# Out-projection rows of a head spread over the units of a slot in chunks one, two and four, and the next chunk's input loaded from ScalarE's queue

## Chip, cores and metric

One core of a Trainium2 chip. The metric is the device time of one execution in microseconds, as the median over the runs of the kernel.

## The reference

x is 2048 tokens by 512, float32. xn is x with LayerNorm. The result is x + attention(xn) + ffn(xn). The attention has 16 heads, a latent of rank 128 shared by keys and values, and a rotary part of 64:

```
q = xn @ wq.T                      # per head 128 nope + 64 rotary
kv = xn @ wkv_a.T                  # 128 latent + 64 rotary key
q_lat = q_nope @ wkv_b[h, :128]    # per head, into the latent
kv_cache = rmsnorm(kv_lat, kv_norm_w)
scores = (q_lat @ kv_cache.T + q_pe @ k_pe.T) * SCALE, causal
out_lat = softmax(scores) @ kv_cache
out = (out_lat @ wkv_b[h, 128:]) of all heads @ wo.T
ffn = xn @ w_ste.T + bias          # w_ste: ternary weight times its mean size
```

## The kernel before, in words

`build_prepare` makes, chunk by chunk, the transposed input, keys and values, the linear part and the products of the weights (Wq for a head's latent query, Wp for the rotary part of a pair of heads, Wv for value times output), and stores xT, the linear part with the residual (acc), Wq, Wp and Wv in scratch memory. `build_attention` is where the change lies. Every factor is held as a high and a low part, so each product is three matmuls (five for scores).

**Order of the work.** There are four chunks of 512 query tokens (NCH = 4, four blocks of 128 rows each, QB = 4), and in each chunk 16 heads (H = 16): 64 heads g, written out in full. A head works in slots. In chunks one and two a slot s is a whole head (s = g, s = 0 to 31); in chunks three and four a head takes two slots of two row blocks each (s = 32 to 95). The functions at the head of the file (L128 to L209) give each piece of work its slot and its unit. A slot has rows times chunk number units: 4 in chunk one, 8 in chunk two, 6 in chunk three, 8 in chunk four. In every unit every engine runs through the same list, so the order on each queue is fixed, and engines meet through semaphores.

**One unit on TensorE** (`slot` in `block.tensor`): `scores` of one row block against 512 keys into one of three p_score buffers (L1106, mask at L1110); `project_rotary` (L1086, p_rot) for the heads g+1 and g+2 if the slot opens an odd head (in chunk one ahead of the scores); `project_latent` parts (L1086, p_lat) of the next head; `project_out` (L1138, p_result), the out-projections of head s-2 or s-3, one per row block; `values` (L1126, p_out), the PV product of slot s-2 in groups. `project_out` of row i waits until row i-2 has been accumulated, since p_result has two buffers, and for row 0 for Wv (`wv_in`) and for o_l of the head (`o_split`).

**VectorE**: `copy_scores` (L1178, with maxima, L1184), `turn_row` (L1200, 32 by 32 transposes of a row after its exp), `rotate` (L1212, L1216, five operations on p_rot), `split_query` (L1223), `split_output` (L1227), `accumulate` (L1241, acc). **ScalarE**: `exp_row` (L1283), `high_group` (L1304), `high_output` (L1310), `high_query` (L1321), `high_rotary` (L1328), and the DMA issues of the last quarter of an exchange (L1293) and of Wq (L1315). **GpSimd**: `add_rotary` (L1369), `low_rotary` (L1378, L1381), `low_group` (L1389).

**SyncE** (`block.sync`) issues, in each slot s in this order: two quarters of the exchange of slot s-1 (L991: eight DMAs of transposed probabilities from turned to pT, after the last `turn_row`), Wp (L998) in slots that open an odd head, in chunk one the load of Wv for the next head (L1003), the third quarter of the exchange (four DMAs), and from slot 16 on the load of Wv here. At the end of a slot that closes head 14 of a chunk come the tables of the next chunk (L1013, L1014) and xT (L1008), at the end of one that closes head 1 of a chunk the store of the chunk before (L1018) and the load of the residual of this one (L1023). `load_v` of head g+1 waits until all four rows of head g are projected. xT, Wq, Wp, Wv and acc have one buffer each. A wait on SyncE holds everything behind it.

The out-projections of a head stand: in chunk one in unit 1, all four rows, in slot g+3; in chunk two in units 6, 6, 7, 7 of slot g+2; in chunk three in units 2 to 5; in chunk four in units 0, 1, 2, 2.

Of the kernel before, what the change touches and what calls it, by code (L numbers as in the profile page):

```python
# [32 lines left out]
H = 16  # L33
# [123 lines left out]
def out_heads(s):  # L157

    if s < H:
        return (s - 3,) if s >= 3 else ()  # L160
    if s < 2 * H:
        return (s - 3, s - 2) if s == H else (s - 2,)
    if s == 2 * H + 1:
        return (2 * H - 2,)
    return (s // 2 + H - 2,) if s % 2 == 0 and s > 2 * H else ()


def out_unit(s, g, i):
    if s < H:
        return 1  # L170
    if s < 2 * H:
        return 0 if g == s - 3 else 6 + i // 2
    return 0 if s % 2 else (2 + i if phase(s) == 2 else (0, 1, 2, 2)[i])
# [14 lines left out]

def rotate_ops(s, u):
    if phase(s) == 0:  # L190
        return range(5) if u == 0 else ()
    first = rotary_unit(s) + 1
    return ((0,), (1, 2), (3, 4))[u - first] if first <= u <= first + 2 else ()


def rotary_unit(s):
    return 1 if phase(s) == 3 else 0


def rotary_add_unit(s):  # L200
    return (1, 4, 4, 5)[phase(s)] if opens_head(s) else None


def rotary_high_unit(s):
    return (2, 5, 5, 6)[phase(s)] if opens_head(s) else None
# [680 lines left out]
def build_attention(nc, t, keep, stored):  # L886
    with ExitStack() as ctx:
# [95 lines left out]
        def _(sp):  # L983
# [21 lines left out]
            def load_chunk(j):  # L1005

                sp.wait_ge(lat_projected, H * j)
                sp.dma_start(xT[:, :, :, :].bitcast(F32), t["xT_scr"][j]).then_inc(xT_in, 16)  # L1008

# [15 lines left out]
            def slot(s):  # L1025
                if 1 <= s <= SLOTS:
                    exchange(s - 1, (0, 1))
# [8 lines left out]
                if s < SLOTS and closes_head(s):  # L1036
                    j, h = chunk_of(head_of(s)), head_of(s) % H
                    if j + 1 < NCH and h == H - 2:
                        load_tables(j + 1)
                        load_chunk(j + 1)  # L1040
# [4 lines left out]
            def load_next_v(s):  # L1045
                for g in out_heads(s):
                    if g + 1 < HEADS:
                        load_v(g + 1)
# [14 lines left out]
        def _(pe):  # L1063
# [77 lines left out]
            def slot(s):  # L1141
                g = head_of(s) if s < SLOTS else HEADS
                for u in range(units_of(s)):
                    rotary = u == rotary_unit(s) and opens_head(s) and g % 2 and g + 1 < HEADS
# [24 lines left out]
        def _(dve):  # L1169
# [75 lines left out]
            def slot(s):  # L1245
                g = head_of(s) if s < SLOTS else HEADS
                for u in range(units_of(s)):
# [9 lines left out]
                    if opens_head(s) and g % 2 and g + 1 < HEADS:  # L1257
# [19 lines left out]
        def _(act):  # L1277
# [33 lines left out]

            def load_q(g):
# [18 lines left out]
            def slot(s):  # L1331
                g = head_of(s) if s < SLOTS else HEADS
                for u in range(units_of(s)):
# [9 lines left out]
                    if u == query_unit(s) and g + 1 < HEADS:  # L1343
                        high_query(g + 1)
                        if g + 2 < HEADS:
                            load_q(g + 2)
                    if u == rotary_high_unit(s) and g + 1 < HEADS:
# [7 lines left out]
            for i in range(2):  # L1355
                act.wait_ge(stored["wq"][i], 16 * H // 2)
            load_q(1)
# [138 lines left out]
```

## Time and profile before

| | |
|---|---|
| median of 3 runs | 1896.98 us |
| lowest, highest | 1886.88, 1898.66 us |
| the profiled execution, its own time | 1894.48 us |
| its span, first to last instruction | 1892.0 us |
| mean granted TensorE clock | 0.969 |
| TensorE, VectorE, ScalarE, GpSimd busy | 91%, 64%, 45%, 53% |

The profile is of one execution. Times in its rows are microseconds from the span's start. The four chunks of attention begin at about 190, 450, 800 and 1260 us; what lies before is `build_prepare`, which the change does not touch.

### The profile page before, as it was taken

What the parts mean: (1) busy time and instruction counts of PE and PEld (TensorE: products, weight loads), DVE (VectorE), ACT (ScalarE), POOL (GpSimd) and SP (SyncE); (2) the same over time, 40 slices, a digit from 0 to 9 for tenths busy, and PEclk for the clock granted to TensorE, in tenths of its full rate; (3) what the DMA queues carried; (4) which work ended last, traced back from release to release, by engine and by line L of the source; (5) the groups of instructions that cost most, each with busy time, mean ns of one, the idle gap of its engine ahead of it and who ended that gap; (6) DMA issues with size and microseconds to landing.
All of it is one profiled execution on the core that took longest, in us unless ns stands there. A gap on an engine that the chain in (4) does not pass through costs nothing.

```text
span 1892.0 us, 28195 instructions
## 1 busy us (share of the span) xinstructions
PE 1717.4 (91%) x9326; PEld 1452.8 (77%) x9326; DVE 1211.1 (64%) x2801; ACT 850.7 (45%) x1358; POOL 1008.2 (53%) x635
## 2 busy tenths in 40 slices
PE   6988788878899999799999999979999999999996
PEld 5877666656778877578888888868888888888875
DVE  4674466655666677466776776657666666666663
ACT  4554334433344454345445445434544544454442
POOL 4674444442365556355655655635555565664654
PEclk9898899988999999899999999989999999999998
DMA  6995355563756656656555554555665564655543
GB/s 201 362 329 198 102 151 146 158 190 101 201 148 174 170 156 163 182 150 179 158 149 145 158 149 135 162 166 143 175 162 130 150 162 119 166 143 130 148 121 105
DMA packets 127184, 309.12 MB, mean 163 GB/s; under 512 B 29442, under 2 KB 41987, under 8 KB 125508
## 3 DMA queue, kind: packets, MB, share of 16 engines
q1 hardware_dynamic: 98720, 233.33, 43.1%
q10 hardware_dynamic: 28324, 74.05, 15.0%
q8 instruction: 72, 1.18, 0.3%
q14 instruction: 68, 0.56, 0.1%
HBM read 113.28 MB, written 34.60 MB: 78 GB/s over the span
## 4 chain that ended last, share of the span: by engine, by line
PE 62%; issue 11%; DVE 7%; POOL 4%; ACT 3%; DMA 1%; SPq 1%; ACTq 1%; POOLq 0%; DVEq 0%
PE p_score L1106 25%; PE p_out L1126 18%; PE p_result L1138 7%; PE p_lat L1086 7%; PE p_rot L1086 5%; POOL pT L1389 2%; DVE acc L1241 2%; DVE turned L1200 2%; ACT qp_h L1328 1%; DVE rot_sin L1216 1%; DVE probs L1178 1%; SPq L991 1%; POOL qp_l L1378 1%; POOL qp_l L1381 1%; PE p_score L1110 1%
## 5 line engine op out<-in xcount | busy, mean ns | idle before, releaser
L1389 POOL TENSOR_TENSOR pT<-pT,pT_h 128x1024 fp32r<-128x1024 f32 x320 | 688.6, 2178 | 445.5 <-ACT pT_h L1304 442.8
L1178 DVE TENSOR_SCALAR_CACHE_REDUCE probs<-p_score 128x512 f32<-128x512 f32 (+3 forms) x640 | 383.6, 602 | 433.6 <-PE p_score L1106 256.8
L1283 ACT ACTIVATE probs<-probs,neg_max 128x128 f32<-128x128 f32 (+15 forms) x256 | 307.9, 1203 | 453.8 <-DVE neg_max L1184 430.3
L1304 ACT ACTIVATE pT_h<-pT 128x1024 fp32r<-128x1024 f32 x320 | 291.1, 963 | 267.3 <-PE p_out L1126 203.6
L1200 DVE STREAM_TRANSPOSE turned<-probs 128x1024 f32<-128x1024 f32 (+7 forms) x384 | 341.8, 915 | 43.2 <-ACT probs L1283 38.5
L1126 PE MATMUL p_out<-pT_h,V_h 128*128 128x256 f32 (+3 forms) x1024 | 303.4, 296 | 18.7 <-POOL pT L1389 18.7
L1126 PE MATMUL p_out<-pT,V_h 128*128 128x256 f32 (+3 forms) x1024 | 302.7, 296 | 0.0
L1126 PE MATMUL p_out<-pT_h,V_l 128*128 128x256 f32 (+3 forms) x1024 | 302.3, 295 | 0.0
L1106 PE MATMUL p_score<-Kp,qp_h 128*128 128x512 f32 (+3 forms) x640 | 235.9, 369 | 15.6 <-POOL qp_l L1381 15.6
L1106 PE MATMUL p_score<-Kn_h,q_h 128*128 128x512 f32 (+3 forms) x640 | 240.3, 375 | 2.4 <-DVE q_l L1223 2.4
L1138 PE MATMUL p_result<-Wv,o_h 128*128 128x512 f32 x512 | 173.8, 421 | 70.9 <-DVE acc L1241 51.4
L1106 PE MATMUL p_score<-Kn_l,q_h 128*128 128x512 f32 (+3 forms) x640 | 234.9, 367 | 0.0
L1106 PE MATMUL p_score<-Kn_h,q_l 128*128 128x512 f32 (+3 forms) x640 | 234.4, 366 | 0.0
L1106 PE MATMUL p_score<-Kp,qp_l 128*128 128x512 f32 (+3 forms) x640 | 233.6, 365 | 0.0
L1086 PE MATMUL p_lat<-xT,Wq 128*128 128x512 f32 x768 | 225.2, 410 | 0.0
L1126 PEld LDWEIGHTS p_out<-pT_h,V_h 128*128 128x128 f32 x1024 | 196.7, 192 | 35.7 <-issue 18.7
L1126 PEld LDWEIGHTS p_out<-pT_h,V_l 128*128 128x128 f32 x1024 | 196.4, 192 | 13.1
L1241 DVE SCALAR_TENSOR_TENSOR acc<-p_result,inv_sum,acc 128x512 f32<-128x512 f32 x256 | 184.6, 745 | 28.5 <-PE p_result L1138 20.7
L1126 PEld LDWEIGHTS p_out<-pT,V_h 128*128 128x128 f32 x1024 | 196.1, 192 | 4.2
L1378 POOL TENSOR_TENSOR qp_l<-rotated,qp_h 64x512 fp32r<-64x512 f32 x64 | 82.3, 1285 | 196.6 <-ACT qp_h L1328 192.7
L1138 PEld LDWEIGHTS p_result<-Wv,o_h 128*128 128x128 f32 x512 | 89.9, 194 | 111.4 <-DVE acc L1241 68.3
L1086 PEld LDWEIGHTS p_lat<-xT,Wq 128*128 128x128 f32 x768 | 142.1, 195 | 25.0
(135 smaller groups left out, 2384.7 us busy)
## 6 DMA issues: line engine op xcount, KB each, us to landing
pT<-turned SPq DMA_DIRECT2D x384, 128.0 KB, 3.6
Wq<-wq_scr ACTq DMA_DIRECT2D x63, 512.0 KB, 4.8
Wv<-wv_scr SPq DMA_DIRECT2D x63, 512.0 KB, 3.5
pT<-turned SPq DMA_DIRECT2D x192, 112.0 KB, 3.8
pT<-turned SPq DMA_DIRECT2D x192, 96.0 KB, 2.9
pT<-turned ACTq DMA_DIRECT2D x128, 128.0 KB, 3.9
Wp<-wp_scr SPq DMA_DIRECT2D x31, 512.0 KB, 4.4
pT<-turned SPq DMA_DIRECT2D x192, 80.0 KB, 2.6
```

The lines of the kernel that those rows point to most:

```text
L991: sp.dma_start(slots(pT[s % 2][32 * a:32 * (a + 1), :], s)[:, r, 0:tiles, :, :].bitcast(F32), slots(turned[s % 2][32 * r:32 * (r + 1), :], ...
L1086: mm = pe.matmul(out, weights[:, w, it, :], xT[:, x, it, :], start=(it == 0 and k == 0), stop=(it == IT - 1 and k == 2))
L1106: mm = pe.matmul(out[:, 0:width], q[p][:, rows], kk[:, keys], start=(k == 0), stop=(k == 4 and b < j))
L1126: mm = pe.matmul(out[:, :, cols, :], v[:, t, :], pt[:, :, t - first, rest, :], start=(t == 0 and a == 0), stop=(t == piece_tiles(s) - 1 an ...
L1138: mm = pe.matmul(out[:, :], o[:, rows], Wv[:, w, :], start=(k == 0), stop=(k == 2))
L1178: dve.tensor_scalar(probs[row % ROW_RING][:, b * CW:b * CW + width], p_score[n % SCORE_RING][:, 0:width], SCALE, LOWEST, ALU.mult, ALU.max ...
L1200: last = dve.transpose(to.rearrange("p a t q -> p t a q"), rows.rearrange("p (t a q) -> p t a q", a=4, q=32))
L1241: dve.scalar_tensor_tensor(out=acc[:, i, :], in0=p_result[(QB * g + i) % 2][:, :], scalar=inv_sum[g % 4][:, i:i + 1], in1=acc[:, i, :], op ...
L1283: act.activation(probs[row % ROW_RING][:, 0:width], probs[row % ROW_RING][:, 0:width], ACT.Exp, bias=neg_max[p][:, i:i + 1], scale=1.0, ac ...
L1304: act.activation(high.rearrange("p r t i q -> p r t (i q)"), low.bitcast(F32).rearrange("p r t i q -> p r t (i q)"), ACT.Copy).then_inc(p_ ...
L1378: pool.tensor_tensor(qp_l[p][0:ROPE, :], rotated[own, :], qp_h[p][own, :].bitcast(F32), ALU.subtract).then_inc(qp_ready, 1)
L1389: pool.tensor_tensor(low.rearrange("p r t i q -> p r t (i q)"), low.bitcast(F32).rearrange("p r t i q -> p r t (i q)"), high.bitcast(F32). ...
```

## The change

Out-projection rows of a head are given other units: chunk one 1, 1, 2, 3 instead of 1, 1, 1, 1; chunk two units 6 and 7 of slot g+2 and units 0 and 1 of slot g+3 instead of 6, 6, 7, 7 (so `out_heads` names two heads in slots 16 to 31, slot 32 gets the last two rows of head 29, and Wv is asked for by the slot of the last row); chunk four 0, 1, 3, 4 instead of 0, 1, 2, 2. The rotary projection moves to unit 2 in chunk three (3 in slot 62, the last before chunk four), and to unit 1 in slots 15 and 31; the operations that follow it move along, in chunk three partly into the next slot. xT of the next chunk is loaded by ScalarE right behind the Wq load of the next chunk's first head, instead of by SyncE at the end of the slot of head 14, and the tables are loaded at the start of that head's first slot.

```diff
@@ out_heads
     if s < 2 * H:
-        return (s - 3, s - 2) if s == H else (s - 2,)
+        return s - 3, s - 2
+    if s == 2 * H:
+        return (2 * H - 3,)
     if s == 2 * H + 1:
@@ out_unit
     if s < H:
-        return 1
-    if s < 2 * H:
-        return 0 if g == s - 3 else 6 + i // 2
-    return 0 if s % 2 else (2 + i if phase(s) == 2 else (0, 1, 2, 2)[i])
+        return (1, 1, 2, 3)[i]
+    if s == H and g == s - 3:
+        return i // 2
+    if s <= 2 * H:
+        return (None, None, 0, 1)[i] if g == s - 3 else (6, 7, None, None)[i]
+    return 0 if s % 2 else (2 + i if phase(s) == 2 else (0, 1, 3, 4)[i])
@@
+def rotary_unit(s):
+    return (1 if s == H - 1 else 0, 1 if s == 2 * H - 1 else 0, 3 if s == 4 * H - 2 else 2, 1)[phase(s)] if opens_head(s) else None
+
 def rotate_ops(s, u):
+    if not opens_head(s):
+        return ()
     if phase(s) == 0:
-        return range(5) if u == 0 else ()
+        return range(5) if u == rotary_unit(s) else ()
     first = rotary_unit(s) + 1
+    if s == 4 * H - 2:
+        return ((0, 1), (2, 3, 4))[u - first] if first <= u <= first + 1 else ()
     return ((0,), (1, 2), (3, 4))[u - first] if first <= u <= first + 2 else ()
-def rotary_unit(s):
-    return 1 if phase(s) == 3 else 0
 def rotary_add_unit(s):
-    return (1, 4, 4, 5)[phase(s)] if opens_head(s) else None
+    if phase(s) == 2:
+        return 0 if not opens_head(s) else None
+    return rotary_unit(s) + (1, 4, None, 4)[phase(s)] if opens_head(s) else None
 def rotary_high_unit(s):
-    return (2, 5, 5, 6)[phase(s)] if opens_head(s) else None
+    if phase(s) == 2:
+        return 1 if not opens_head(s) else None
+    return rotary_unit(s) + (2, 5, None, 5)[phase(s)] if opens_head(s) else None
@@ block.sync
-            def load_chunk(j):
-
-                sp.wait_ge(lat_projected, H * j)
-                sp.dma_start(xT[:, :, :, :].bitcast(F32), t["xT_scr"][j]).then_inc(xT_in, 16)
             def slot(s):
+                if opens_head(s) and head_of(s) % H == H - 2 and chunk_of(head_of(s)) + 1 < NCH:
+                    load_tables(chunk_of(head_of(s)) + 1)
...
                     j, h = chunk_of(head_of(s)), head_of(s) % H
-                    if j + 1 < NCH and h == H - 2:
-                        load_tables(j + 1)
-                        load_chunk(j + 1)
                     if j and h == 1:
                         store_chunk(j - 1)
                         load_residual(j)
             def load_next_v(s):
                 for g in out_heads(s):
-                    if g + 1 < HEADS:
+                    if g + 1 < HEADS and out_unit(s, g, QB - 1) is not None:
                         load_v(g + 1)
@@ block.scalar
+            def load_chunk(j):
+
+                act.wait_ge(lat_projected, H * j)
+                act.wait_ge(rot_projected, H // 2 * j)
+                act.dma_start(xT[:, :, :, :].bitcast(F32), t["xT_scr"][j]).then_inc(xT_in, 16)
...
                         if g + 2 < HEADS:
                             load_q(g + 2)
+                        if (g + 2) % H == 0 and g + 2 < HEADS:
+                            load_chunk(chunk_of(g + 2))
...
+            act.wait_ge(stored["xT"], 16 * (NCH - 1))
             load_q(1)
```

In `block.tensor` and `block.vector` the test for the slot of an odd head is adapted to the new `rotary_unit`; nothing else changes there.

## Rows read from the trace of the kernel before

**Rows 1.** The page's head and view 1, busy time and share of the span

```profile
span 1892.0 us, 28195 instructions
...
PE 1717.4 (91%) x9326; PEld 1452.8 (77%) x9326; DVE 1211.1 (64%) x2801; ACT 850.7 (45%) x1358; POOL 1008.2 (53%) x635
```

**Rows 2.** TensorE's waits over the whole span: us in total, times, longest us

```profile
PE p_result L1138 <- DVE acc L1241: 51.4, 49, 3.2
PE p_rot L1086 <- issue: 29.5, 3, 11.2
```

**Rows 3.** Stretches: us, then PE, PEld, DVE, ACT, POOL busy, PEclk, DMA, GB/s

```profile
354.00:384.50 30.50, 25.86 (x133) 20.60 (x133) 20.01 (x51) 12.73 (x28) 13.67 (x10) 1.00 0.57 156
384.50:417.20 32.70, 28.38 (x133) 22.56 (x131) 20.11 (x52) 12.80 (x28) 13.21 (x9) 0.90 0.54 147
562.80:604.40 41.60, 40.01 (x198) 33.08 (x197) 29.14 (x68) 20.32 (x32) 23.23 (x14) 1.00 0.61 164
```

**Rows 4.** A rotary projection in the chain of waits; then TensorE in chunk one

```profile
353.95 2.81 PE p_rot L1086 x12
...
363.90 0.73 PE L1138 MATMUL p_result<-Wv,o_h 128*128 128x512 f32 x2 [3.03 <-DVE acc L1241]
...
372.48 0.33 PE L1106 MATMUL p_score<-Kp,qp_h 128*128 128x128 f32 x1 [1.06 <-POOL qp_l L1381]
```

**Rows 5.** VectorE in the same slot (timeline)

```profile
359.73 2.79 DVE L1216 TENSOR_TENSOR rot_sin<-p_rot,sinT_sb 32x512 f32<-32x512 f32 x4
```

**Rows 6.** GpSimd in chunk one, odd slot and even slot (timeline)

```profile
363.82 3.65 POOL L1389 TENSOR_TENSOR pT<-pT,pT_h 128x1024 fp32r<-128x1024 f32 x2
...
378.57 3.65 POOL L1389 TENSOR_TENSOR pT<-pT,pT_h 128x1024 fp32r<-128x1024 f32 x2 [6.14 <-ACT pT_h L1304]
```

**Rows 7.** SyncE in an even slot of chunk two, and TensorE at row 0

```profile
625.36 0.33 SPq L1003 DMA_DIRECT2D Wv<-wv_scr  x1
629.18 9.12 SPq L991 DMA_DIRECT2D pT<-turned  x12
...
639.73 0.62 PE L1138 MATMUL p_result<-Wv,o_h 128*128 128x512 f32 x2
```

**Rows 8.** TensorE's waits in chunk two, 470 to 770

```profile
PE p_result L1138 <- DVE acc L1241: 12.7, 15, 1.4
PE p_out L1126 <- POOL pT L1389: 4.5, 1, 4.5
```

**Rows 9.** DMA issues, median us to landing: all Wv; one Wp

```profile
Wv<-wv_scr SPq DMA_DIRECT2D x63, 512.0 KB, 3.5
...
Wp<-wp_scr SPq DMA_DIRECT2D x1, 512.0 KB, 6.9
```

**Rows 10.** SyncE at the store of chunk one; ScalarE waiting for an exchange

```profile
494.73 0.40 SPq L1018 DMA_DIRECT2D out<-acc  x1
...
500.21 9.37 SPq L991 DMA_DIRECT2D pT<-turned  x12
...
518.59 2.95 ACT L1304 ACTIVATE pT_h<-pT 128x1024 fp32r<-128x1024 f32 x3 [8.40 <-DMA pT<-turned]
```

**Rows 11.** XT issues (SyncE), Wq issues (ScalarE), p_rot, third and fourth chunk

```profile
771.31 0.43 SPq L1008 DMA_DIRECT2D xT<-xT_scr  x1
...
1232.77 0.43 SPq L1008 DMA_DIRECT2D xT<-xT_scr  x1
...
763.91 0.34 ACTq L1315 DMA_DIRECT2D Wq<-wq_scr  x1
...
1227.31 0.35 ACTq L1315 DMA_DIRECT2D Wq<-wq_scr  x1
...
782.33 4.67 PE L1086 MATMUL p_rot<-xT,Wp 128*128 128x512 f32 x12 [11.25 <-issue]
...
1244.46 5.46 PE L1086 MATMUL p_rot<-xT,Wp 128*128 128x512 f32 x12 [9.32 <-issue]
```

**Rows 12.** TensorE in an even slot of chunk four (timeline)

```profile
1425.26 0.73 PE L1138 MATMUL p_result<-Wv,o_h 128*128 128x512 f32 x2 [0.94 <-DVE acc L1241]
```

More of the change, by code:

```diff
@@ L1143, in slot @@
                 for u in range(units_of(s)):
-                    rotary = u == rotary_unit(s) and opens_head(s) and g % 2 and g + 1 < HEADS
+                    rotary = u == rotary_unit(s) and g % 2 and g + 1 < HEADS
                     if rotary and s < H:
@@ L1256, in slot @@
                             split_output(old)
-                    if opens_head(s) and g % 2 and g + 1 < HEADS:
+                    if g % 2 and g + 1 < HEADS:
                         for op in rotate_ops(s, u):
```

## The prediction

> **What bounds the kernel now.** I read the busy shares first, then TensorE's own waits, then TensorE's timeline of one steady pair of heads in each chunk, and only then the queues. TensorE is busy 91% of a span of 1892.0 us [rows 1], so only its idle time and its slow stretches can be won. Its two largest waits are both touched by the change [rows 2]: the out-projection waits for VectorE's accumulate (51.4 us, 49 times), and the rotary projection waits at the three chunk changes for xT (29.5 us in 3 waits; the releaser reads "issue" because it is a DMA). The first has one cause everywhere: p_result has two buffers, and four rows are projected in one or two units, so row 2 needs row 0 accumulated. A third cost is the clock: two neighbouring pairs of chunk one take 30.5 us at clock 1.00 and 32.7 us at 0.90 [rows 3], so a dip costs 2.2 us.
>
> I call a slot with a rotary projection odd, the other even. Twelve 512-column matmuls take 2.81 us [rows 4], so 0.23 us each: one out row 0.7 us, one full score unit 1.15 us.
>
> **Part 1, chunk one, rows at units 1, 1, 2, 3.** In the odd slot TensorE waits 3.03 us for acc and ends by waiting 1.06 us for qp_l at the next head [rows 4]. VectorE gets to the accumulates only after the rotate operations, whose four rot_sin alone hold it from 359.73 for 2.79 us [rows 5]. That order stays. TensorE now does score 2 and two latent parts (2.4 us) before row 2, so of 3.03 us about 0.8 is left. But then comes the PV product, and its pT is not there: GpSimd starts it at 363.82, 3.65 us for two groups [rows 6], so the first is usable at about 366.2 against TensorE's 364.6: 1.6 us of new wait. The slot ends 0.9 us sooner, the next head's qp_l, whose chain hangs on latent parts finished 4 us sooner but behind pT on GpSimd, comes 1.6 us sooner. In the even slot the wait before row 2 was 0.2; row 3 leaves the stretch ahead of the PV product, and pT (start 378.57, behind ScalarE's exchange issues [rows 6]) is then 1.6 us late instead of 0.3. Per pair: 1.6 won, 0.7 given back, 0.9 net; six pairs give -5.5. If pT is not the next limit, 3.2 per pair. Wv is asked for later, at unit 3, with 4 us before its use; the middle landing of Wv is 3.5 us [rows 9]: I allow +2. Three pairs had a dip of 2.2; gaps half as long should spare half: -3.5. Sum -7, bounds -20 and +6.
>
> **Part 2, chunk two, rows at units 6, 7, 0, 1.** The 12.7 us of acc waits in this chunk [rows 8] go. But Wv has one buffer. Before, its load was issued at the end of a slot (625.36) and had 14 us until row 0 at unit 6 (639.73). Now head g ends at unit 1 of the slot after, and SyncE asks for Wv of g+1 behind the exchanges, which begin at 629.18 and take 9.12 us to issue [rows 7]. VectorE reaches the transpose that releases them about 1.4 us sooner than now (one accumulate fewer ahead of it, then ScalarE's last exp sets it): 627.8 + 9.1 = 636.9, and Wv lands L later. Row 0 is due at 639.73 less the acc wait of 0.73 that went, 639.0. Even slots wait L - 2.1; odd slots, 2.5 us longer but with Wp to issue too, L - 4 less the wait before them. L: the median of all Wv loads is 3.5 us; a 512 KB load on SyncE's queue between exchanges (Wp) took 6.9 [rows 9]. I take 4.3, nearer the first, since all exchanges are issued before it and only the last are still moving: 2.2 us in each even slot, none in odd ones. Five steady even slots and slot 17: 11.5 - 12.7 = -1, bounds -7 and +26 (at L = 6.9 both kinds of slot wait, 6.4 us per pair).
>
> **Part 3, slot 18.** store_chunk(0) stands at the end of SyncE's slot 17 and waits for all 64 accumulates. Rows 2 and 3 of head 15 now come in slot 18, units 0 and 1, so the store goes from 494.73 to about 498.8. Behind it on SyncE's queue: residual, twelve exchanges (from 500.21 for 9.37 us), then Wv for head 16. The exchanges landed at 518.6, when ScalarE's 8.40 us wait ended [rows 10], and cost TensorE 4.5 us [rows 8]. Now they land about 4 us later, and Wv, which head 16 needs at unit 6 (about 508), comes with or after them, at about 522. TensorE stands 14 us, then does 8.4 us of work, some of it at the low clock (+3), up to where it stood before at 524: +10, bounds +3 and +16. This stall takes the place of the wait of 4.5.
>
> **Part 4, xT from ScalarE's queue.** Before, xT stood on SyncE behind Wv and tables: issued 771.31 and 1232.77, in use 782.33 and 1244.46 [rows 11]: about 11 us. The new place is right behind the Wq load, which ScalarE issued at 763.91 and 1227.31 [rows 11]. ScalarE's own waits cost nothing: both counts stand when Wq is issued.
> Into the third chunk: xT lands at about 775 (11 us). The rotary comes at unit 1, after a score and an out row, and with the Wv wait of slot 30 it is due at about 772. Before it began at 782.33: -7.3, and its slow product (4.67 us against 2.81) probably a normal one: -8.5 in all; bounds -4 and -10.
> Into the fourth chunk: landing 1238 to 1240; the rotary moves from unit 0 to unit 3 of slot 62, three scores and an out row later, due 1235.1 + 4.3 = 1239.4. The 9.3 us go, and 5.46 becomes about 2.8: -11.5, bounds -6 and -12.
> Into the second chunk: Wq and xT go out only 2 us sooner. Wait 29.5 - 11.2 - 9.3 = 9.0 shrinks to about 5: -3.8. In the same slot 15 an acc wait of 3 us and half a dip go, since the rotary sits later: -4.5. Together -8, bounds -2 and -11.
> The exchange DMAs that now queue behind xT on ScalarE are needed a slot later: nothing. The tables are asked for a slot sooner on SyncE, idle then: nothing.
> In sentences of their own: the Trainium skill, "DMA: Bandwidth & Descriptors", section "Issuing engines are not separate DMA queues", says that transfers issued from different engines run on the same 16 engines and interleave, so that a second queue saves only the issue time. By it the exchanges, which stood behind xT on one queue, now take a share beside it, and the sum would be rival B's; by the rows above it is mine.
>
> **Part 5, rotary of chunk three from unit 0 to 2.** Same products, still ahead of row 0; VectorE's rotate operations fall among accumulates and end about 2 us later; exchanges 1.5 us later, with about 2 us of slack ahead of PV. The o_l waits (1.2 us per pair) are not touched. 0, bounds -2 and +8.
>
> **Part 6, chunk four, rows at units 0, 1, 3, 4.** Even-slot waits of 0.94 [rows 12] and 0.3 per pair. Unit 3's score is narrow (0.55 us), so row 2 still waits about 0.5: 0.75 won in each of seven pairs, and 1 at the chunk's start: -6.5, bounds -10 and 0. One 0.7 wait in slot 32: -0.7.
>
> **Sum.** -7 - 1 + 10 - 8.5 - 11.5 - 8 - 6.5 - 0.7 = -33.2. Waits removed one by one tend to come back in part: in this schedule SyncE's issue time fills most of a slot, and I worked out only the next-latest cause. I take three quarters, -25 (my choice, from no row). The profiled execution took 1894.48 us, the median of three is 1896.98: 1897 - 25 = 1872 us.
>
> **Rivals.**
> A. The forecast: 1872.
> B. xT from ScalarE lands late because SyncE's exchanges move beside it instead of behind it. At xT's rate (2 MB in 11 us) the up to 1.5 MB of twelve exchanges are 8 us of transfer; half of it in xT's way makes 15 us, and the three chunk changes win 2, 4.5 and 6 less: 1872 + 12.5 = 1885. For it: twelve exchanges are being issued from before 1227 on. Against: they are issued 0.75 us apart and land in 3 to 4 us, so they leave gaps.
> C. The other side: Wv is late all through chunks one and two. It decides at L = 4.7: from there odd slots wait too, and each later us is paid twice per pair. At 6.9 chunk two gives +26 instead of -1, chunk one loses 2.8 per pair, +17, and slot 18 comes to its upper bound, +6: 1872 + 50 = 1922; at 5.5 about 1890. For it: Wp among exchanges took 6.9; against: the load is the last on its queue.
> D. The Wv load is nearly in time (L = 3.3: 5 less) and slot 18 costs its lower bound (7 less): 1872 - 12 = 1860.
> E. The accumulates are not what holds the out rows, and qp_l or pT hold chunk one wholly: it gives nothing instead of 15 with slot 15: 1887.
>
> **Chances.** A 0.48, B 0.17, C 0.12, D 0.10, E 0.13. Under 1% (19 us, 1878) is about what a measurement of this kernel can tell from no change; A lies 6 us beyond it, so a third of A falls inside. Faster 0.32 + 0.10 + 0.10 (D, and parts of B and E) = 0.52; slower over 1% (from 1916) only C's upper end, 0.06; the rest 0.42. Range 1852 to 1894: it leaves out most of C and the last of D.
>
> **What would show each step.** Chunk one: pairs of 29.6 us instead of 30.5, the 3.03 gone, waits of about 1.6 for pT before PV in both slots. Chunk two: no acc waits, a wait of about 2 us before row 0 in even slots whose releaser is no engine but a DMA, pairs of 42.2 us instead of 41.6 [rows 3]. Slot 18: a single wait of some 14 us before an out-projection. xT: waits of about 5, 2 and 0 us ahead of p_rot, issued by ScalarE's queue. Chunk three: pairs unchanged. Chunk four: 0.5 us left of 1.25. Wrong if the Wv waits exceed 5 us, if slot 18 shows no stall, or if xT waits keep 9 us.

## The result, and the profile after

| | before | changed |
|---|---|---|
| median of 6 runs | 1893.38 us | 1877.46 us |
| lowest, highest | 1886.39, 1898.66 us | 1870.81, 1885.99 us |
| the profiled execution | 1894.48 us | 1875.69 us |
| its span | 1892.0 us | 1873.6 us |
| mean granted TensorE clock | 0.969 | 0.969 |

The ratio is 0.9908, with a 95% interval of 0.9881 to 0.9936: 16 us faster. The forecast was 1872 us in a range of 1852 to 1894.

The head of the page, with the busy shares that answer to [rows 1]:

```profile
span 1873.6 us, 28199 instructions
...
PE 1718.6 (92%) x9326; PEld 1451.6 (77%) x9326; DVE 1212.3 (65%) x2801; ACT 849.0 (45%) x1358; POOL 1008.3 (54%) x635
```

TensorE's waits over the whole span (us in total, times, longest us), which answer to [rows 2]:

```profile
PE p_result L1144 <- issue: 36.8, 18, 13.8
PE p_out L1132 <- POOL pT L1404: 21.0, 14, 6.0
...
PE p_result L1144 <- DVE acc L1247: 14.7, 17, 3.2
...
PE p_rot L1092 <- issue: 7.5, 3, 5.7
```

The matmul work is the same. Both waits that the change aimed at went: acc from 51.4 to 14.7 us, xT from 29.5 to 7.5. That is 58.7 us. Of it 36.8 came back under a name that did not stand among the rows of before, `p_result <- issue`: an out-projection that waits for a DMA, which is Wv. So the first reading is: two big gains, and one new wait that eats over half of them.

Where it stands can be read from the starts of the rotary projections (p_rot), one per pair of heads, in both timelines. The differences between neighbouring marks give a ledger; in chunk three the rotary sits two score units (2.3 us) later in its slot, which is taken off.

| stretch (mark before, mark after) | us | the prediction's term |
|---|---|---|
| up to the first rotary (199.03, 197.20) | -1.8 | none |
| chunk one to slot 13 (384.34, 377.60) | -4.9 | -7 |
| slots 13 to 17, xT of chunk two in it (474.63, 455.92) | -12.0 | -8 |
| slots 17 and 18 (514.24, 515.57) | +20.0 | +10 with slot 17's 2.2 |
| slots 19 and 20 (562.64, 558.03) | -5.9 | |
| slots 21 to 28 (729.27, 733.65) | +9.0 | -3 |
| slot 29 to the second pair of chunk three, xT in it (952.30, 953.85) | -5.1 | -8.5 and 0 |
| steady chunk three (1178.46, 1179.97) | 0.0 | 0 |
| xT of chunk four (1312.01, 1302.54) | -8.7 | -11.5 |
| chunk four (1748.71, 1732.81) | -6.4 | -6.5 |
| tail | -2.5 | none |
| sum | -18.3 | -33.2, taken as -25 |

Each column of marks is one execution. The tail belongs to chunk four: experiment 8 below, which changes chunk four's rows alone, has 2.4 us of it.

**Chunk one.** TensorE in one pair (start, duration, instruction, the wait in brackets), beside [rows 4]; then the stretches of one pair of chunk one, two neighbouring pairs of chunk two and one of chunk four (us, busy of PE, PEld, DVE, ACT, POOL, then PEclk, DMA share, GB/s), beside [rows 3]:

```profile
357.12 0.73 PE L1144 MATMUL p_result<-Wv,o_h 128*128 128x512 f32 x2 [0.63 <-DVE acc L1247]
...
359.56 0.47 PE L1132 MATMUL p_out<-pT_h,V_h 128*128 128x512 f32 x1 [1.48 <-POOL pT L1404]
...
369.02 0.69 PE L1144 MATMUL p_result<-Wv,o_h 128*128 128x512 f32 x2 [1.03 <-issue]
```

```profile
347.00:377.60 30.60, 27.46 (x135) 21.66 (x134) 19.70 (x52) 12.69 (x29) 13.53 (x9) 0.94 0.55 155
...
603.10:645.50 42.40, 40.32 (x198) 32.71 (x197) 29.37 (x69) 20.18 (x33) 23.33 (x14) 1.00 0.61 161
645.50:691.30 45.80, 41.99 (x198) 33.67 (x197) 29.44 (x69) 20.31 (x33) 23.23 (x14) 0.96 0.58 150
1447.15:1518.58 71.43, 70.80 (x410) 61.17 (x408) 49.51 (x110) 34.85 (x43) 42.24 (x21) 1.00 0.59 148
```

The 3.03 us for acc are 0.63, the 1.06 for qp_l are gone, and 1.48 for pT stand in their place, as forecast (0.8, none, 1.6). Not forecast at this size is the 1.03 us before an out row in the even slot: Wv. And the pair takes 30.60 us at a granted clock of 0.94, where the 30.50 of [rows 3] were taken at 1.00: the pair has fewer waits, and part of it ran at the 1.2 GHz level, which pays the gain away. Both are single pairs; experiment 6 has the sums over the chunk.

**Chunk two.** Row 0 of the out-projections, in slots 17 and 18, and then in four neighbouring slots, 21 to 24:

```profile
475.66 1.19 PE L1144 MATMUL p_result<-Wv,o_h 128*128 128x512 f32 x2 [4.98 <-issue]
...
509.91 0.77 PE L1144 MATMUL p_result<-Wv,o_h 128*128 128x512 f32 x1 [13.79 <-issue]
...
578.20 0.81 PE L1144 MATMUL p_result<-Wv,o_h 128*128 128x512 f32 x2 [2.66 <-issue]
...
598.67 0.70 PE L1144 MATMUL p_result<-Wv,o_h 128*128 128x512 f32 x2 [0.27 <-issue]
...
622.13 0.70 PE L1144 MATMUL p_result<-Wv,o_h 128*128 128x512 f32 x2 [1.51 <-issue]
...
641.06 0.70 PE L1144 MATMUL p_result<-Wv,o_h 128*128 128x512 f32 x2 [0.31 <-issue]
```

The long waits (2.66, 1.51, then 3.31 in slot 25) are in the odd slots, the short ones (0.27, 0.31) in the even ones. The prediction had it the other way round. The landings in one odd slot, 560 to 580 (issues: out and in, queue, KB, median us to landing), beside [rows 9]:

```profile
Wp<-wp_scr SPq DMA_DIRECT2D x1, 512.0 KB, 7.6
Wv<-wv_scr SPq DMA_DIRECT2D x1, 512.0 KB, 6.6
```

Slot 18 on SyncE's queue, and ScalarE's next work, beside [rows 10]; then the stretch in which TensorE stands:

```profile
485.73 0.40 SPq L1025 DMA_DIRECT2D out<-acc  x1
491.86 0.34 SPq L1030 DMA_DIRECT2D acc<-acc_scr  x1
492.30 8.00 SPq L1003 DMA_DIRECT2D pT<-turned  x12
500.34 0.59 SPq L1015 DMA_DIRECT2D Wv<-wv_scr  x1
```

```profile
500.00:506.00 6.00, 0.00 (x0) 0.00 (x0) 0.00 (x0) 0.00 (x0) 0.16 (x1) 0.51 1.03 215
```

Store, residual and twelve exchanges stand in front of Wv, as forecast. Wv is issued at 500.34 and row 0 starts at 509.91, 9.6 us later, with the DMA engines full. In that stall TensorE, VectorE and ScalarE do nothing, and the granted clock falls to 0.51.

**xT.** The issues in the second and third of the three changes (ScalarE's queue), and the rotary projections behind all three, beside [rows 11]:

```profile
770.50 0.52 ACTq L1322 DMA_DIRECT2D xT<-xT_scr  x1
...
1227.70 0.64 ACTq L1322 DMA_DIRECT2D xT<-xT_scr  x1
```

```profile
414.75 4.59 PE L1092 MATMUL p_rot<-xT,Wp 128*128 128x512 f32 x12 [5.71 <-issue]
...
778.85 4.46 PE L1092 MATMUL p_rot<-xT,Wp 128*128 128x512 f32 x12 [1.65 <-issue]
...
874.68 0.73 PE L1144 MATMUL p_result<-Wv,o_h 128*128 128x512 f32 x2 [2.54 <-DVE acc L1247]
...
1240.14 3.00 PE L1092 MATMUL p_rot<-xT,Wp 128*128 128x512 f32 x12 [0.18 <-issue]
...
1415.44 0.73 PE L1144 MATMUL p_result<-Wv,o_h 128*128 128x512 f32 x2 [0.40 <-DVE acc L1247]
```

Waits of 5.7, 1.65 and 0.2 us, forecast as 5, 2 and 0. In the same fence stand an accumulate wait of 2.54 us in chunk three's second pair, which was 0.79 before and belongs to no term, and chunk four's 0.40 that is left of 0.94 [rows 12].

### The profile page after: what moved, and what is told of

Read it like the earlier page. It is cut to its first block and busy times, and to the rows that moved or that the text cites. A ratio compares the mean times of both kernels' runs of the same rounds, so it can differ in the third digit from the quotient of the medians.

```text
span 1873.6 us, 28199 instructions
## 1 busy us (share of the span) xinstructions
PE 1718.6 (92%) x9326; PEld 1451.6 (77%) x9326; DVE 1212.3 (65%) x2801; ACT 849.0 (45%) x1358; POOL 1008.3 (54%) x635
## 3 DMA queue, kind: packets, MB, share of 16 engines
q10 hardware_dynamic: 28756, 80.35, 15.7%
## 5 line engine op out<-in xcount | busy, mean ns | idle before, releaser
L1144 PE MATMUL p_result<-Wv,o_h 128*128 128x512 f32 x512 | 175.7, 425 | 71.9 <-issue 36.8
L1247 DVE SCALAR_TENSOR_TENSOR acc<-p_result,inv_sum,acc 128x512 f32<-128x512 f32 x256 | 189.2, 744 | 74.6 <-PE p_result L1144 63.4
```

The lines of the kernel that those rows point to most:

```text
L1144: mm = pe.matmul(out[:, :], o[:, rows], Wv[:, w, :], start=(k == 0), stop=(k == 2))
L1247: dve.scalar_tensor_tensor(out=acc[:, i, :], in0=p_result[(QB * g + i) % 2][:, :], scalar=inv_sum[g % 4][:, i:i + 1], in1=acc[:, i, :], op ...
```

## The experiments

The theory after the result, W: chunk two's spread is what costs, because it makes the load of Wv late (one buffer, asked for behind twelve exchanges, and in slot 18 behind the store too); everything else brings what it should. The rivals: E, that with Wv in time pT and qp_l would hold TensorE just as long; and that the gains of the other parts are not theirs but the later place's or the clock's. The kernels carry their edit against the kernel named; the kernel before took 1891.8 to 1895.4 us (medians) in the runs beside them.

**1. Chunk two's spread taken back.**

```diff
 # against the changed kernel, out_heads and out_unit
-    if s < 2 * H:
-        return s - 3, s - 2
-    if s == 2 * H:
-        return (2 * H - 3,)
+    if s < 2 * H:
+        return (s - 3, s - 2) if s == H else (s - 2,)
...
-    if s <= 2 * H:
-        return (None, None, 0, 1)[i] if g == s - 3 else (6, 7, None, None)[i]
+    if s < 2 * H:
+        return 6 + i // 2
```

> The changed kernel with chunk two's out rows back at units 6, 6, 7, 7 of slot g+2; all other parts of the change stay. Theory W (Wv asked for behind the exchanges, and the store of chunk one one slot later, cost chunk two about 23 us between slot 17 and the third chunk): about 1854 us, no wait of p_result for a DMA above 1 us from slot 17 on, acc waits of 0.7 to 0.9 us back in each slot. Rival R (chunk two loses time because of something else in the change, xT or the rotary on ScalarE's queue): 1877 us or more, since then only the acc waits come back (+12).

Measured: 1850.26 us (1843.13 to 1852.98), ratio to before 0.9779, 0.9729 to 0.9828. By the medians that is 27 us under the changed kernel, by the ratios 24, and between the rotary projections of slots 13 and 29 the two traces differ by 24 us (332.1 for 356.1), so most of it lies where the edit is. Its stretches, a pair of chunk one and one of chunk two:

```profile
343.40:372.20 28.80, 25.95 (x134) 20.53 (x134) 19.69 (x52) 12.71 (x29) 13.84 (x10) 1.00 0.57 165
579.30:621.00 41.70, 40.09 (x197) 33.08 (x196) 29.17 (x69) 20.34 (x33) 23.23 (x14) 1.00 0.61 164
```

Chunk two is back at 41.7 us a pair with acc waits of 0.74 and 0.87. Chunk one's code and waits are those of the changed kernel (0.63 for acc, 1.48 for pT, 0.59 to 0.95 for Wv), yet its pair takes 28.80 us instead of 30.60, and what differs beside some 0.4 us of the wait for Wv (0.59 for 1.03) is the clock, 1.00 instead of 0.94. So the spread of chunk one is worth 1.7 us a pair at the full clock ([rows 3] has 30.50), and the changed kernel's profiled execution did not get it in four of the six pairs. The profiled execution here, 1843 us, is the fastest of its four.

**2. Chunk two's spread alone, on the kernel before** (the same lines the other way, and Wv asked for by the slot of the last row).

> The kernel before with chunk two's spread alone. Theory W: 23 us slower than before (1893), about 1916. Rival R: within 5 us of before.

Measured: 1910.78 us (1904.46 to 1919.58), ratio 1.0085, 1.0056 to 1.0114: slower than before by some 16 us. Its waits in slots 17 and 18:

```profile
499.31 1.19 PE L1142 MATMUL p_result<-Wv,o_h 128*128 128x512 f32 x2 [4.93 <-issue]
...
531.63 1.19 PE L1142 MATMUL p_result<-Wv,o_h 128*128 128x512 f32 x2 [10.88 <-issue]
```

Added or taken away, the part costs: 16 us alone, some 24 to 27 among the others. The traces show where the difference can come from. Alone, slots 13 to 29 take 365.9 us for 344.9, 21 more, and behind them the wait for xT at the third chunk is 3.52 us instead of 11.25: TensorE comes to it later, and so waits less. In the changed kernel that wait is short in any case, so there is little to get back.

**3. Wv asked for first.**

```diff
 # against the changed kernel, SyncE's slot(s)
+                if H <= s <= 2 * H:
+                    load_next_v(s)
                 if 1 <= s <= SLOTS:
                     exchange(s - 1, (0, 1))
...
-                if s >= H:
+                if s > 2 * H:
                     load_next_v(s)
```

> The changed kernel, with SyncE asking for Wv at the start of slots 16 to 32, ahead of the exchange; the spread stays. Theory W: the waits of row 0 for Wv vanish in the steady slots of chunk two, pairs of 40.1 us instead of 42.4 to 45.8; in slot 18 the store and the residual still stand ahead of Wv, so a stall of about 4 us stays there instead of 13.8. In all about 1845 us. Rival R: the waits are not Wv's place in the queue (DMA engines too busy), then pairs stay above 42 and the time at 1870 or more. Rival E: the exchange, now behind the wait for out row 3, comes late and the PV product waits for pT instead: pairs of 41 to 43, 1860.

Measured: 1859.41 us (1857.26 to 1862.48), ratio 0.9823, 0.9772 to 0.9873. Row 0 in slot 18, and a PV product in the slot behind it:

```profile
495.98 1.19 PE L1146 MATMUL p_result<-Wv,o_h 128*128 128x512 f32 x2 [4.50 <-issue]
...
508.44 0.47 PE L1134 MATMUL p_out<-pT_h,V_h 128*128 128x512 f32 x1 [1.38 <-POOL pT L1406]
```

The steady Wv waits are gone and slot 18's is 4.50 instead of 13.79. But pT waits of 0.2 to 1.4 us turn up in five of the slots from 18 on, and one of 3.30 us in slot 17, since the exchanges now stand behind Wv, and the time stays 14 us over what was expected. Steady pairs take 41.7 to 42.8 us, no less than the 41.6 of [rows 3]. W holds for Wv, and E is real too: with acc and Wv out of the way the exchange is the next limit.

**4. The same, and slot 18 cleared**: the store behind Wv, the residual behind the first eight exchanges.

```diff
 # against experiment 3, SyncE's slot(s)
+                if s == H + 2:
+                    store_chunk(0)
                 if 1 <= s <= SLOTS:
                     exchange(s - 1, (0, 1))
+                if s == H + 2:
+                    load_residual(1)
...
-                    if j and h == 1:
+                    if j > 1 and h == 1:
```

> As the kernel before this one, and the store of chunk one goes to slot 18 behind Wv, the residual of chunk two behind the first eight exchange DMAs of that slot. Theory W: no stall above 1 us at the out-projection of slot 18; the exchange of slot 17 lands on time or 1 to 2 us late: about 1840 us, 5 us below the kernel before this one. Rival: the slot's DMA traffic (1 MB store, 1 MB residual, 2 MB exchange, Wq and Wv) is the limit in any order, then a wait of 4 us or more stays somewhere in slots 18 and 19 and the time is that of the kernel before this one.

Measured: 1856.15 us (1849.94 to 1858.54), ratio 0.9796, 0.9743 to 0.9848. No row waits for Wv in slot 18, but the PV products beside it wait 3.81 and 1.85 us for pT. Of the two orders tried, neither is better than leaving the spread out (1850.26); other orders were not tried.

**5. Wp moved to the even slots**, to settle the parity: is the odd slot's Wv late because Wp's 512 KB go in front of it?

```diff
 # against the changed kernel, SyncE's slot(s)
-                if opens_head(s) and head_of(s) % 2 and head_of(s) + 3 < HEADS:
+                if H < s < 2 * H - 1:
+                    if s % 2 == 0:
+                        load_rotary(s + 2)
+                elif opens_head(s) and head_of(s) % 2 and head_of(s) + 3 < HEADS:
                     load_rotary(head_of(s) + 3)
```

> The changed kernel (1877 us), with the Wp load of chunk two's steady slots (17 to 29, odd) issued in the even slot behind it, at the same place between the exchanges; Wv's wait is there in both. Theory Wp (Wv is late because it is queued behind Wp's 512 KB in the odd slots: waits before row 0 of 1.3 to 3.3 us in odd slots and 0.2 to 0.5 in even ones): the parity turns over, odd slots 0 to 0.5 us, even slots 1.5 or more (they are also 2.5 us shorter, so up to 4), and the time stays at 1877 or goes up to 1885. Rival: the odd slots are late for another reason (VectorE's rotate operations push the last transpose, the exchanges and so Wv back); then they keep 1.3 to 3.3 us, even slots get longer waits too, and the time is 1885 or more. Other side: if no slot waits, 1865.

Measured: 1890.51 us (1879.83 to 1896.59), ratio 0.9983, 0.9962 to 1.0005. Row 0 in slot 22; SyncE's queue before it; the landings of 575 to 592:

```profile
597.33 1.19 PE L1147 MATMUL p_result<-Wv,o_h 128*128 128x512 f32 x2 [4.83 <-issue]
```

```profile
580.50 6.00 SPq L1003 DMA_DIRECT2D pT<-turned  x8
586.54 0.62 SPq L1010 DMA_DIRECT2D Wp<-wp_scr  x1
587.26 2.41 SPq L1003 DMA_DIRECT2D pT<-turned  x4
589.71 0.59 SPq L1015 DMA_DIRECT2D Wv<-wv_scr  x1
```

```profile
Wp<-wp_scr SPq DMA_DIRECT2D x1, 512.0 KB, 7.6
Wv<-wv_scr SPq DMA_DIRECT2D x1, 512.0 KB, 7.5
```

The parity turned over: the even slots 20 to 30 wait 2.0 to 4.8 us, no odd slot waits. So the wait goes with the load of Wp, and the rival, VectorE's rotate operations in the odd slots, falls. The landing time alone does not explain it, though: the 7.5 above is the longest of its kind. In this kernel Wv lands in 4.7 to 7.5 us behind Wp and in 4.5 to 6.2 without it, while in the changed kernel, slots 19 to 30, it was 6.3 to 7.3 behind Wp and 3.5 to 4.1 without. Here the slot that has Wp is also the shorter one, by the prediction's 2.5 us. Why Wv takes over 4 us here with no Wp before it was not settled.

The time came out above the expected 1877 to 1885, 13 us over the changed kernel. Between the rotary projections of slots 19 and 29 it takes 229.6 us for 218.1. For the same products TensorE is busy 211.9 us for 204.9 (granted clock 0.95 for 0.98), and it waits 15.7 us for Wv in 5 waits for 11.4 in 8. So 7 of these 11.5 us are the clock, behind fewer and longer waits.

**6. Chunk one's spread taken back too.**

```diff
 # against experiment 1, out_unit
-        return (1, 1, 2, 3)[i]
+        return 1
```

> The changed kernel with chunk two's rows back at units 6, 6, 7, 7 (c2_undone, 1850 us), and chunk one's rows back in unit 1 as well. Theory P, the spread of chunk one gives what its pairs show at clock 1.00: 28.9 us instead of 30.5, 1.6 us in each of six pairs, and here too no dip adds to it: 1860 us, with the waits of 3.03 us for acc and 1.06 for qp_l back. Rival E (of the prediction), the spread gives nothing: 1850, since pT and Wv hold TensorE as long as acc did. Rival clock: the row waits are long gaps after which the clock drops; then about 2 us more per pair, 1866 or over, with a granted clock in 229:377 under that of c2_undone (0.99).

Measured: 1860.54 us (1858.13 to 1866.01), ratio 0.9824, 0.9803 to 0.9845: 10 us over experiment 1. The old waits are back:

```profile
364.25 0.94 PE L1142 MATMUL p_result<-Wv,o_h 128*128 128x512 f32 x2 [3.03 <-DVE acc L1245]
...
374.38 0.33 PE L1110 MATMUL p_score<-Kp,qp_h 128*128 128x128 f32 x1 [1.08 <-POOL qp_l L1394]
```

By the medians the spread of chunk one gives 10 us, as theory P said; the intervals of the two ratios overlap a little (0.9729 to 0.9828, 0.9803 to 0.9845), so the traces have to bear it out. From the rotary projection of slot 1 to that of slot 13 the profiled executions of the seven kernels here with rows at 1, 1, 2, 3 took 173.6 to 181.3 us, 178.2 in the mean. Those of the five with all rows in unit 1 (this one, before, experiments 2, 7 and 8) took 185.3 to 191.9, mean 187.8. The two groups do not overlap, and the means differ by 9.6 us. The forecast's rival E, that the spread gives nothing, falls. The kernel before had the shortest time of its group, 185.3, which is why the ledger shows only 4.9. What varies within a group is the clock: in this kernel it was 1.00 in one of the six pairs and 0.88 to 0.95 in the others, in experiment 1 it was 1.00 in five. So the rival that the clock takes part is not excluded: between these two traces the six pairs differ by 14.5 us, where 1.7 us in each pair at the full clock make 10.

**7. xT from ScalarE's queue alone, on the kernel before**, every rotary in its old unit, tables a head earlier (the hunks on `load_chunk` and `load_tables` of the change).

> The kernel before with nothing changed but that ScalarE loads xT behind Wq and that SyncE loads the tables a head earlier; every rotary projection stays in its unit. Theory Q (the queue alone carries part 4 of the prediction): xT lands at about 773 to 775 and 1237 to 1239, the rotaries are due at 771.1 and 1235.1, so waits of about 3 us instead of 11.2 and 9.3; into chunk two little, 2 us: about -16 in all, 1877 us. Rival R (the later place of the rotary carries it): over 6 us of wait stay at each of the three changes, 1886 or above. A landing that the exchanges delay (rival B of the prediction) would show as waits of over 5 us too, with xT issued by 1228.

Measured: 1877.46 us (1870.13 to 1884.43), ratio 0.9905, 0.9881 to 0.9928. The rotary projections behind the three changes:

```profile
427.18 3.25 PE L1080 MATMUL p_rot<-xT,Wp 128*128 128x512 f32 x7 [7.37 <-issue]
...
769.58 2.98 PE L1080 MATMUL p_rot<-xT,Wp 128*128 128x512 f32 x12 [2.38 <-issue]
...
1225.23 4.71 PE L1080 MATMUL p_rot<-xT,Wp 128*128 128x512 f32 x12 [5.62 <-issue]
```

The queue alone brings 18 us, theory Q. The later place of the rotary matters mainly at the fourth chunk, where 5.62 us are left here and 0.18 in the changed kernel; at the other two it is 7.37 for 5.71 and 2.38 for 1.65.

**8. Chunk four's rows alone, on the kernel before.**

```diff
-    return 0 if s % 2 else (2 + i if phase(s) == 2 else (0, 1, 2, 2)[i])
+    return 0 if s % 2 else (2 + i if phase(s) == 2 else (0, 1, 3, 4)[i])
```

> The kernel before with chunk four's rows at units 0, 1, 3, 4 and nothing else. By the prediction's part 6 -6.5 us, by the changed kernel's marks -6.4 in the chunk and -2.5 in the tail: 1885 to 1887 us, pairs of 71.4 instead of 72.63 us and waits of about 0.4 left. Rival: what the changed kernel won in chunk four came from its xT and rotary being a unit further along, and then the pairs keep over 72.2 and the time 1892.

Measured: 1882.65 us (1878.03 to 1885.37), ratio 0.9938, 0.9921 to 0.9954: -13 us by the medians, 9 to 15 by the interval. The waits of chunk four's steady pairs are 0.38 to 0.41 again, so the waits of chunk four are this edit's. Its trace has 7.2 us less than before from the fourth chunk's first rotary projection to its last, and 2.4 less in the tail: 9.6 us, as expected. The rest of the 13 is not shown to come from the edit.

**9. Chunk three's rotary back in unit 0.**

```diff
 # against experiment 1, rotary_unit; the add and high units follow as before
-    return (1 if s == H - 1 else 0, 1 if s == 2 * H - 1 else 0, 3 if s == 4 * H - 2 else 2, 1)[phase(s)] if opens_head(s) else None
+    return (1 if s == H - 1 else 0, 1 if s == 2 * H - 1 else 0, 3 if s == 4 * H - 2 else 0, 1)[phase(s)] if opens_head(s) else None
```

> c2_undone (1850 us) with chunk three's rotary projections back in unit 0 (slot 62 keeps unit 3). By the prediction's part 5 the place of the rotary changes nothing in steady chunk three, pairs 56.5 us either way. Theory S: the 3 us that the changed kernel lost at the start of chunk three (an accumulate wait of 2.54 us instead of 0.79 at 874.7) come from the rotate operations standing among the accumulates, and go: 1847. Rival: nothing changes, 1850. Other side: with rotary at unit 0 the rotate operations stand ahead of row 0's accumulate, as before: also possible 1853.

Measured: 1844.20 us (1842.27 to 1845.28), ratio 0.9731, 0.9714 to 0.9748. Experiment 1 has this wait in chunk three's second pair, and this kernel has none there:

```profile
838.80 0.73 PE L1142 MATMUL p_result<-Wv,o_h 128*128 128x512 f32 x2 [1.92 <-DVE acc L1245]
```

Steady pairs are 56.5 us either way, so the place of the rotary counts only at the start of the chunk. Theory S holds for the wait. From the first rotary projection on the new xT to the fourth pair of the chunk the two traces differ by 1.5 us. The step from 1850 to 1844 by the medians is larger, the ranges and intervals of the two kernels overlap, and the profiled executions are 1843 and 1844: more than some 2 us is not shown.

**10. Chunk one with its last row in unit 2.**

```diff
 # against experiment 9, out_unit
-        return (1, 1, 2, 3)[i]
+        return (1, 1, 2, 2)[i]
```

> c2_rot3_undone (1844 us) with chunk one's rows at units 1, 1, 2, 2 instead of 1, 1, 2, 3. Theory T: row 3 fills 0.7 us of the 1.47 us that the PV product waits for pT in odd slots, and Wv, asked for 2 us sooner, takes the 0.9 us wait out of the even slots: 1.6 us per pair, six pairs and a bit, 1834 us, pairs of 27.4 at clock 1.00. Rival: row 3 waits for the accumulate of row 1 (p_result has two buffers) and pT stays the limit in even slots too, 0.6 per pair or less: 1841 to 1844.

Measured: 1847.57 us (1838.68 to 1852.31), ratio 0.9761, 0.9733 to 0.9789: no gain. The wait for Wv is gone and pT's is 0.80 instead of 1.48, both as theory T said. A wait that neither theory named took their place; TensorE in a slot of chunk one, and the landings of 350 to 372:

```profile
366.43 2.10 PE L1090 MATMUL p_lat<-xT,Wq 128*128 128x512 f32 x6 [1.97 <-DMA Wq<-wq_scr]
```

```profile
Wq<-wq_scr ACTq DMA_DIRECT2D x1, 512.0 KB, 8.2
Wv<-wv_scr SPq DMA_DIRECT2D x1, 512.0 KB, 8.3
```

Wp is issued at 356.22, Wq at 358.21 and Wv at 358.30, so three loads of 512 KB are on the way together and Wq takes 8.2 us. In experiment 9 Wp, Wq and Wv went out at 353.47, 355.47 and 361.16, and Wq's median was 3.9. Wv asked for sooner made Wq late.

**11. xT ahead of Wq.**

```diff
 # against experiment 9, ScalarE's slot(s)
-                            load_q(g + 2)
-                        if (g + 2) % H == 0 and g + 2 < HEADS:
-                            load_chunk(chunk_of(g + 2))
+                            if (g + 2) % H == 0:
+                                load_chunk(chunk_of(g + 2))
+                            load_q(g + 2)
```

> c2_rot3_undone (1844 us) with ScalarE asking for xT ahead of Wq at the three chunk changes instead of behind it. Theory X: xT goes out 0.7 us sooner and without Wq's 512 KB in front of it, and the waits of 5.94 and 3.48 us before the rotary become 3.5 and 1.5 us; Wq lands behind it, under the rotary's own 3 to 5 us: 1840 us. Rival: the two transfers share the 16 engines either way and the exchanges set the landing, waits shrink by under 1 us, or the wait moves to the latent products: 1843 to 1846.

Measured: 1840.87 us (1836.58 to 1842.69), ratio 0.9721, 0.9697 to 0.9745. The first two rotary projections:

```profile
415.41 5.46 PE L1090 MATMUL p_rot<-xT,Wp 128*128 128x512 f32 x12 [2.99 <-issue]
...
752.40 2.97 PE L1090 MATMUL p_rot<-xT,Wp 128*128 128x512 f32 x12 [0.25 <-issue]
```

Waits of 5.94 and 3.48 became 2.99 and 0.25, and no latent product waits for Wq there: theory X. The loads of xT landed in 8.4, 7.9 and 9.2 us, where those of experiment 9, behind Wq, took 10.9, 10.7 and 11.9. The intervals of 9 and 11 overlap, so the 3 us rest on these waits more than on the medians. With experiment 12, which ties with it, this is the fastest kernel here: 2.8% under before, and some 36 us under the changed kernel.

**12. Both edits of 10 and 11.**

> c2_rot3_undone with both edits, chunk one's rows at 1, 1, 2, 2 and xT asked for ahead of Wq: if both theories hold and add up, 1844 - 10 - 4 = 1830 us; if neither, 1844. They touch different stretches (slots 3 to 15, and the three chunk changes), so the gain should be the sum of the two single ones within 2 us.

Measured: 1840.65 us (1838.63 to 1841.32), ratio 0.9722, 0.9700 to 0.9745: that of experiment 11. Its chunk one waits for Wq again (1.66, 0.97, 1.19 and 1.07 us), so the edit of 10 adds nothing.

## Why the prediction was right, and where it was not

Sign and range held: 1877 for 1872. Point by point:

- **Part 1, chunk one, -7.** By the ledger -4.9 in the changed kernel, by experiment 6 some -10. The chain of waits was read rightly (0.8, 0, 1.6 forecast in the odd slot; 0.63, 0, 1.48 measured). Two sizes were off, against each other: pT's forecast wait in the even slot is not there, and Wv's, allowed at 2 us in all, is 0.6 to 1.1 in each pair. What was not in the sum is that a pair with these waits runs at a clock of 1.00 in one execution and 0.94 in another. The 3.5 us that I booked for dips spared were not to be had in this one.
- **Part 2, chunk two, -1: the step that failed**, although its upper bound holds it. Slots 19 to 28 came to +3 by the ledger, -5.9 at the recovery from slot 18 and then +9.0. The formula for Wv was right (ask, plus L, against the due time); its L was not. I took one L of 4.3 for both kinds of slot, "nearer the first, since all exchanges are issued before it", and so put the waits into the short, even slots. Wv behind Wp takes 6.6 us (6.3 to 7.3 over the slots), about as long as the 6.9 of Wp among exchanges in [rows 9] that I had set aside; with L = 6.6 the formula gives 2.6 in the odd slots less the wait before them, where 1.3 to 3.3 were measured; in an even slot Wv landed in 3.9, for which it gives 1.8, and 0.3 was measured. Experiment 5 shows that the wait goes with Wp, though not by the landing time alone. Two more things were off. Five even slots and slot 17 at 2.2 us make 13.2, not the 11.5 of the sum. And the clock was in no term of this part: in slots 21 to 28 the waits are 11.1 us for 6.4, and TensorE is busy 4.2 us longer for the same products (clock 0.98 for 1.00), which together are the +9.0.
- **Part 3, slot 18, +10.** The stall was forecast at 14 us and is 13.79. Slots 17 and 18 cost +20.0, since slot 17 waits 4.98 us for Wv where 2.2 were allowed, and the clock is low around both (0.83 over the two slots, for 1.00 before). With the recovery of 5.9 behind it that is +14.
- **Part 4, xT, -28.** The ledger has -12.0 into the second chunk for -8, and -8.7 into the fourth for -11.5. Into the third the wait fell by 9.6, for a forecast of 8.5, and some 4 us were lost again behind it. Into the second 4.0 of the 12.0 us are less time at the low clock (TensorE busy 64.5 us for 68.6). Rival B falls: it needed a landing of 15 us for xT beside the exchanges, and the three took 10.8, 8.3 and 12.4 us, where before they took 9.5, 10.9 and 11.6. At the fourth chunk it came nearest (12.4, and 12.6 in experiment 7), and the later rotary covers that: TensorE waits 0.18 us for it.
- **Part 5, the rotary of chunk three, 0.** Right for steady pairs, wrong at the start of the chunk, where VectorE has its rotate operations among the accumulates while it is still behind: 2.54 us of acc wait for 0.79, and by the traces of experiments 1 and 9 some 2 us in all.
- **Part 6, chunk four, -6.5.** -6.4 and 2.5 more in the tail, and 0.40 left for 0.5.
- **The sum.** The raw sum was -33, the result -16 to -18. The quarter that I took off, 8 us, had no row behind it, and it covered about half of what parts 2 and 3 were short (+9 forecast, +23 measured). It was right in size for a wrong reason: the waits came back mostly in one place, chunk two. That the total came within 6 us of 1872 is in so far luck, and chunk two's spread, which I priced at -1 with a stall of +10, costs enough that the kernel is better without it.
- **Rival C**, Wv late all through, is what happened in part: its condition, L over 4.7, was met in the odd slots alone, and it got 0.12 where [rows 9] had the number.
- **Rival E** was priced at 15 us, part 1's 7 and the whole 8 of the second chunk; but 3.8 of those 8 are xT's and not the accumulates'. It falls by experiment 6 in either case.

The parts by themselves add up only roughly: -18 (xT), -10 (chunk four, by its trace), -10 (chunk one), +16 (chunk two alone) and +2 (chunk three's rotary) make -20 for a measured -16; with the 24 that chunk two costs among the others it is -12.

The Trainium skill, "DMA: Bandwidth & Descriptors", section "Issuing engines are not separate DMA queues", says that another issuing engine saves only the time to initiate a DMA, and calls that usually small beside the transfer. The first half agrees with the landings here, which grow whichever queue the neighbours are on: in experiment 10 Wq on ScalarE's queue takes 8.2 us with Wp and Wv on SyncE's beside it, and 3.9 in experiment 9. The second holds for one transfer and not for a queue of them: an exchange DMA takes SyncE 0.67 us to issue and lands in 3.4, but twelve take 8.00 us to issue. What xT gained by the other queue is the work that stood ahead of it: before, it was issued 7.4 and 5.5 us after Wq [rows 11], in experiment 7 0.4 and 0.7 us after it.

## What to carry to other kernels

When rows that share a single-buffered weight are spread over more time, the weight's next load moves with the last row: work out its due time from the queue it will stand in, with the landing time that the nearest load has among the same neighbours, not with the median of all loads. A wait that the change moves ahead of a once-only event (a store and a residual at a chunk change) has to be priced there by itself. And after each wait removed look for the next load that now goes out beside another: Wv beside Wp and Wq beside Wv cost here what the accumulate had cost, or more.

## What the runs showed of the hardware that I had not expected

- A 512 KB load landed in 3.9 us (Wv and Wq in experiment 9, chunk one), in 6.3 to 7.3 with Wp issued 4.1 to 4.7 us before it (changed kernel, slots 19 to 29), and in 8.2 with two other such loads beside it (experiment 10).
- The same instructions with the same waits of at most 1.5 us ran one pair of chunk one in 28.8 us at a granted clock of 1.00 (experiment 1) and in 30.6 at 0.94 (the changed kernel). Which of the two a pair gets was not settled; the same kernel has both in one execution.
- In the 6 us in which TensorE stood still in slot 18 the granted clock was 0.51, the 1.2 GHz level, and the first rotary products behind the longer waits for xT took 4.5 to 5.5 us instead of 3.0.
